# Gated delta-rule scan: squared lengths of keys and queries summed into the bank of alpha and beta, both transposed raw, and GpSimd's products moved to other tokens

## The reference

```python
q = _l2norm((x @ Wq).reshape(b, s, H, D)) / math.sqrt(D)
k = _l2norm((x @ Wk).reshape(b, s, H, D))
v = (x @ Wv).reshape(b, s, H, D)
dt = softplus(x @ Walpha + dt_bias)
alpha = exp(-exp(A_log) * dt)
beta = sigmoid(x @ Wbeta)

def step(state, inp):
    q_t, k_t, v_t, a_t, b_t = inp
    state = a_t[..., None, None] * state
    stored = einsum('bhij,bhj->bhi', state, k_t)
    delta = b_t[..., None] * (v_t - stored)
    state = state + einsum('bhi,bhj->bhij', delta, k_t)
    return state, einsum('bhij,bhj->bhi', state, q_t)
```

## Time and profile before

| what | value |
|---|---|
| median of the runs | 2251.55 us (2251.38 to 2252.23) |
| profiled execution: its time, its span | 2256.53 us, 2254.7 us |
| busy in the span: PE, DVE, ACT, POOL | 74%, 80%, 66%, 59% |
| first and last chain instruction of the scan | 31.5 us, 606.0 us |
| mean granted TensorE clock | 0.844 |

### The profile page before, as it was taken

One profiled execution on the slowest core, in us unless ns is written; L12 is line 12 of the kernel. 1 busy time (PEld: TensorE's weight loads), 2 busy tenths in 40 slices (PEclk: granted clock), 3 DMA queues, 4 the chain that ended last, 5 costly groups with the idle time before them and its releaser, 6 DMA issues. The chain is left out here.

```text
span 2254.7 us, 51777 instructions
## 1 busy us (share of the span) xinstructions
PE 1673.6 (74%) x16844; PEld 1360.7 (60%) x16844; DVE 1794.9 (80%) x4769; ACT 1480.4 (66%) x3849; POOL 1335.4 (59%) x1497
## 2 busy tenths in 40 slices
PE   5778777787654599993899999999987469997000
PEld 2555555455552388882788888888877258886000
DVE  6999999999878677785899999999957957776221
ACT  5787878788544577771788888888873747775000
POOL 3555556565500355533899999999870045553774
PEclk8888888888756699995999999999985679998555
DMA  1001010010340033331111111111102013333322
GB/s 35 15 15 29 15 29 21 22 29 10 95 146 19 27 81 80 82 72 33 26 29 31 31 30 31 31 31 31 27 8 75 0 49 80 81 82 64 80 77 56
DMA packets 145827, 101.59 MB, mean 45 GB/s; under 512 B 22144, under 2 KB 134688, under 8 KB 145568
## 3 DMA queue, kind: packets, MB, share of 16 engines
q1 hardware_dynamic: 110880, 54.20, 8.7%
q0 software_dynamic: 17408, 35.69, 6.9%
q10 hardware_dynamic: 17280, 8.40, 1.3%
HBM read 53.63 MB, written 35.65 MB: 40 GB/s over the span
## 5 line engine op out<-in xcount | busy, mean ns | idle before, releaser
L1067 POOL DMA_INDIRECT ffn_xs<-normed,ffn_tokeni x288 | 274.2, 952 | 450.6 <-DVE posi L1444 252.5
L1854 POOL TENSOR_TENSOR att_pl<-att_p,att_ph 128x384 f16<-128x384 f32 x512 | 454.6, 916 | 53.6 <-ACT att_ph L2075 45.3
L326 POOL TENSOR_TENSOR sq<-states,qS 128x256 f32<-128x256 f32 x256 | 243.0, 949 | 236.9 <-DVE states L754 235.0
L573 ACT ACTIVATE decayed<-states,alpha 128x64 f32<-128x64 f32 x1024 | 272.1, 336 | 107.4 <-DVE states L754 105.4
L1274 ACT ACTIVATE ffn_h<-bank,b_cols 128x256 f32<-128x256 f32 x576 | 226.1, 474 | 129.6 <-PE bank L1162 118.7
L2182 DVE TENSOR_REDUCE att_mx<-bank 128x3 f32<-128x384 f32 x512 | 279.6, 551 | 36.3 <-PE bank L1911 32.5
L2072 ACT ACTIVATE att_p<-bank 128x384 f32<-128x384 f32 x512 | 252.0, 492 | 57.1 <-PE bank L1948 54.3
L403 PEld LDWEIGHTS bank<-sq,ident 128*128 128x128 f32 x1024 | 225.6, 251 | 46.0 <-issue 26.7
L2075 ACT ACTIVATE att_ph<-bank 128x384 f16<-128x384 f32 x512 | 253.3, 495 | 0.0
L403 PE MATMUL bank<-sq,ident 128*128 128x128 f32 x1024 | 247.7, 413 | 3.3 <-POOL sq L326 3.3
L1175 PE MATMUL bank<-w_h,ffn_hh 128*128 x1152 | 226.0, 224 | 12.7 <-issue 3.8
(11 more groups left out here) (340 smaller groups left out, 5057.8 us busy)
## 6 DMA issues: line engine op xcount, KB each, us to landing
slots<-ffn_ys SPq DMA_DIRECT2D x144, 128.0 KB
normed<-ffn_xn ACTq DMA_DIRECT2D x32, 256.0 KB, 2.3
att_qz<-att_qp SPq DMA_DIRECT2D x256, 32.0 KB
ffn_xs<-normed,ffn_tokeni POOLq DMA_INDIRECT x288
xin<-in_x SPq DMA_DIRECT2D x64, 64.0 KB, 2.0
xres<-in_x SPq DMA_DIRECT2D x64, 64.0 KB, 2.0
x<-x SPq DMA_DIRECT2D x64, 64.0 KB, 1.8
x_all<-x SPq DMA_DIRECT2D x8, 512.0 KB, 4.8
```

Source lines behind the costliest of these rows:

```text
L326: nc.gpsimd.tensor_tensor(sq[:, t, :].rearrange("p (h i j) -> p h i j", h=HL, i=D), states[:, t, :].rearrange("p (h i j) -> p h i j", h=HL ...
L573: ins = nc.scalar.activation(decayed[:, 64 * h:64 * h + 64], states[:, (t - 1) % TC, 64 * h:64 * h + 64], ACT.Copy, scale=alpha[p][:, t, h ...
L1067: pool.indirect_dma_start(xs[j % AHEAD][:, r, :], None, A["normed"], bass.IndirectOffsetOnAxis(ap=tokeni[:, BR * j + r:BR * j + r + 1], ax ...
L1854: nc.gpsimd.tensor_tensor(pl[:, h % RP, :], p32[:, h % RP, :], ph[:, h % RP, :], ALU.subtract).then_inc(low_done, 1)
```

## The change

**Norms.** The two matmuls into full banks are gone. `pick_k` and `pick_q` are 128x128 matrices with one column for each head, so the squared lengths land in the columns of the alpha and beta bank that were empty (each group's 32 hold 4 alpha, 4 beta, now 4 k and 4 q). dt_bias is added there too, by a matmul of one row. One transpose (`ab_scan`) brings all four. ScalarE's relu and logarithm then work on 128x128, its two exponentials on 128x64.

**Keys and queries** are transposed unscaled, straight from PSUM. The lengths enter through GpSimd: beta_k = minus_beta x krinv, beta_kk = beta_k x krinv, beta_v uses beta_k, mab uses beta_kk, and the new product q_scaled (128x512) scales the queries. z, minus_z and minus_abs_z on VectorE become one Abs on ScalarE and a factor -1 in the exponential.

**Places.** Nearly all slots move; gate goes from step 15 of the chunk before to step 5 of its own.

```diff
-    ab_scan=24, z=25, minus_z=26, minus_abs_z=27, z_pos=29, v_scan=28, u_plus_2=33, u_rec=34, beta_den=35, minus_beta=36,
-    s=37, s2=38, h15=39, h13=41, h11=42, h9=43, k_unit=44, h7=45, h5=46, h3=47, k_scan=48, log1p=49, dt=50,
-    decay_log=51, gate_log=52, q_unit=56, q_scan=60)
+    xn=16, v_scan=22, k_scan=24, q_scan=28, ab_scan=32, z_pos=33, u_plus_2=36, u_rec=37, beta_den=38, minus_beta=39,
+    s=40, s2=41, h15=42, h13=43, h11=44, h9=45, h7=46, h5=47, h3=48, log1p=49, dt=50, decay_log=51, gate_log=52)
...
-PREP_ACT_STEP = dict(xT=0, x_sq=1, x_log=2, x_rinv=3, k_sq=5, q_sq=6, u=7, beta_exp=7, k_relu=8, k_log=9, k_rinv=10,
-                     gate_abs=10, gate_exp=11, q_relu=11, gate_ln=12, q_log=12, q_rinv=13, alpha=13, gate_sig=14, gate_rows=15)
+PREP_ACT_STEP = dict(xT=0, x_sq=1, x_log=2, x_rinv=3, k_sq=5, q_sq=6, z_abs=8, u=8, beta_exp=8, n_relu=9, n_log=9,
+                     k_rinv=9, q_rinv=9, gate_abs=10, gate_exp=11, gate_ln=12, alpha=13, gate_sig=14, gate_rows=15)
-POST_ACT_STEP = dict(o_sq=5, o_log=8, o_rinv=9, x1=14)
+POST_ACT_STEP = dict(o_sq=5, o_log=7, o_rinv=7, x1=14)
-PREP_POOL_STEP = dict(beta_v=11, minus_alpha_beta=14, k_scaled=14, gate=15)
+PREP_POOL_STEP = dict(beta_k=10, beta_kk=10, beta_v=11, q_scaled=12, minus_alpha_beta=13, k_scaled=13)
+GATE_STEP = 5
-POST_POOL_STEP = dict(o_unit=9, o_gated=10)
+POST_POOL_STEP = dict(o_unit=8, o_gated=9)
...
-            def k_norm(i, p):
+            def decays_and_norms(i, p):
                 c = 2 * i + p
+                if c == 0:
+                    pe.wait_ge(picked, 2)
+                nc.tensor.matmul(ps_t[:, :], wab[:, :], xn[:, :], start=True, stop=False)
+                nc.tensor.matmul(ps_t[:, :], dt_row[:, :], ones_row[:, :], start=False, stop=False)
                 pe.wait_ge(prep_act, prep_at(PREP_ACT, c, "k_sq"))
-                pe.wait_ge(prep_dve, prep_at(PREP, c, "v_scan"))
-                nc.tensor.matmul(ps_n[:, :], head_ones[:, :], ksq[:, :], start=True, stop=True).then_inc(prep_pe, 1)
-
-            def q_norm(i, p):
-                c = 2 * i + p
-                pe.wait_ge(prep_act, prep_at(PREP_ACT, c, "k_relu"))
-                nc.tensor.matmul(ps_n[:, :], head_ones[:, :], qsq[:, :], start=True, stop=True).then_inc(prep_pe, 1)
+                nc.tensor.matmul(ps_t[:, :], pick_k[:, :], ksq[:, :], start=False, stop=False)
+                pe.wait_ge(prep_act, prep_at(PREP_ACT, c, "q_sq"))
+                nc.tensor.matmul(ps_t[:, :], pick_q[:, :], qsq[:, :], start=False, stop=True).then_inc(prep_pe, 1)
...
                 if ahead(i, p):
+                    decays_and_norms(*ahead(i, p))
                     gates(*ahead(i, p))
-                    k_norm(*ahead(i, p))
-                    q_norm(*ahead(i, p))
...
-                elif name == "k_unit":
-                    act_did("k_rinv")
-                    ins = v.tensor_tensor(kE[:, :], ps_k[:, :], krinv[:, :], ALU.mult)
                 elif name == "k_scan":
-                    need("k_unit")
-                    ins = v.transpose(kS[p][:, :], kE[:, :])
+                    act_did("k_sq")
+                    ins = v.transpose(kS[p][:, :], ps_k[:, :])
...
                 elif name == "q_scan":
+                    act_did("q_sq")
+                    ins = v.transpose(qR[:, :], ps_q[:, :])
```

More of the change, by code:

```diff
@@ L144, in scan @@
         outer = ps_d[:, HL * D:HL * D + SD]
-        poly, polyb, urec = (held(HL * D + SD + n * TC * HL) for n in range(3))
-        nz, dtt = urec, polyb
+        poly, dtt, urec = (held(HL * D + SD + n * TC * HL) for n in range(3))
         alpha, mab = ([sb(f"{n}{p}", [P, TC, HL]) for p in range(2)] for n in ("alpha", "mab"))
@@ L275, in prep @@
                 g = nc.gpsimd
[L276 to L281, removed]
+                if name == "beta_k":
+                    pool.wait_ge(prep_dve, prep_at(PREP, c, "minus_beta"))
+                    pool.wait_ge(prep_act, prep_at(PREP_ACT, c, "q_rinv"))
+                    ins = g.tensor_tensor(bk[:, :, :], mbeta[:, :, :], krinv[:, :, :], ALU.mult)
+                elif name == "beta_kk":
+                    pool.wait_ge(prep_pool, prep_at(PREP_POOL, c, "beta_k"))
+                    ins = g.tensor_tensor(bkk[:, :, :], bk[:, :, :], krinv[:, :, :], ALU.mult)
+                elif name == "q_scaled":
+                    pool.wait_ge(prep_dve, prep_at(PREP, c, "q_scan"))
+                    ins = g.tensor_tensor(qS[p][:, :].rearrange("p (th i) -> p th i", i=D),
+                                          qR[:, :].rearrange("p (th i) -> p th i", i=D),
+                                          qrinv[:, :, :].rearrange("p t h -> p (t h)").unsqueeze(2)
+                                          .to_broadcast([P, TC * HL, D]), ALU.mult)
                 elif name == "beta_v":
-                    pool.wait_ge(prep_dve, prep_at(PREP, c, "minus_beta"))
+                    pool.wait_ge(prep_pool, prep_at(PREP_POOL, c, "beta_k"))
                     ins = g.tensor_tensor(prod[p][:, :, :, D].rearrange("p t (h i) -> p (t h) i", i=D),
                                           vS[:, :].rearrange("p (th i) -> p th i", i=D),
-                                          mbeta[:, :, :].rearrange("p t h -> p (t h)").unsqueeze(2)
+                                          bk[:, :, :].rearrange("p t h -> p (t h)").unsqueeze(2)
                                           .to_broadcast([P, TC * HL, D]), ALU.mult)
@@ L290, in prep @@
                     pool.wait_ge(prep_act, prep_at(PREP_ACT, c, "alpha"))
-                    ins = g.tensor_tensor(mab[p][:, :, :], alpha[p][:, :, :], mbeta[:, :, :], ALU.mult)
+                    pool.wait_ge(prep_pool, prep_at(PREP_POOL, c, "beta_kk"))
+                    ins = g.tensor_tensor(mab[p][:, :, :], alpha[p][:, :, :], bkk[:, :, :], ALU.mult)
                 else:
@@ L298, in prep, with gate @@
                 ins.then_inc(prep_pool, 1)
+            def gate(i, p):
+                c = 2 * i + p
+                pool.wait_ge(prep_act, prep_at(PREP_ACT, c, "gate_rows"))
+                if c >= 2:
+                    pool.wait_ge(post_pool, prep_at(POST_POOL, c - 2, "o_gated"))
+                nc.gpsimd.tensor_tensor(gE[p][:, :], gR[:, :], gsig[:, :], ALU.mult).then_inc(gated, 1)
             def post(name, i, p):
@@ L329, in chunk @@
                         qb.to_broadcast([P, HL, D, D]), ALU.mult).then_inc(sq_ready, 1)
+                    if t == GATE_STEP:
+                        gate(i, p)
                     if behind(i, p):
@@ L621, in prep @@
                     ins = v.transpose(aS[:, :], ps_t[:, :])
-                elif name == "z":
-                    need("ab_scan")
-                    ins = v.tensor_tensor(z[:, :, :], aview[:, :, 0:HL], hl(dt_bias[:, :]), ALU.add)
-                elif name == "minus_z":
-                    need("z")
-                    ins = v.tensor_scalar(nz[:, :, :], z[:, :, :], -1.0, None, ALU.mult)
-                elif name == "minus_abs_z":
-                    need("minus_z")
-                    ins = v.tensor_tensor(nab[:, :, :], z[:, :, :], nz[:, :, :], ALU.min)
-                elif name == "k_unit":
-                    act_did("k_rinv")
-                    ins = v.tensor_tensor(kE[:, :], ps_k[:, :], krinv[:, :], ALU.mult)
-                elif name == "k_scan":
-                    need("k_unit")
-                    ins = v.transpose(kS[p][:, :], kE[:, :])
-                elif name == "q_unit":
-                    act_did("q_rinv")
-                    ins = v.tensor_tensor(qE[:, :], ps_q[:, :], qrinv[:, :], ALU.mult)
+                elif name == "k_scan":
+                    act_did("k_sq")
+                    ins = v.transpose(kS[p][:, :], ps_k[:, :])
                 elif name == "q_scan":
-                    need("q_unit")
-                    if not (isinstance(c, int) and c < 2):
-                        dve.wait_ge(sq_ready, (c - 1) * TC)
-                    ins = v.transpose(qS[p][:, :], qE[:, :])
+                    act_did("q_sq")
+                    ins = v.transpose(qR[:, :], ps_q[:, :])
                 elif name == "gate_log":
@@ L655, in prep @@
                 elif name == "z_pos":
-                    ins = v.tensor_scalar(zp[:, :, :], z[:, :, :], 0.0, None, ALU.max)
+                    need("ab_scan")
+                    ins = v.tensor_scalar(zp[:, :, :], aview[:, :, 0:HL], 0.0, None, ALU.max)
                 elif name == "u_plus_2":
                     act_did("u")
-                    ins = v.tensor_scalar(u2[:, :, :], u[:, :, :], 2.0, None, ALU.add)
+                    ins = v.tensor_scalar(poly[:, :, :], u[:, :, :], 2.0, None, ALU.add)
                 elif name == "u_rec":
                     need("u_plus_2")
-                    ins = v.reciprocal(urec[:, :, :], u2[:, :, :])
+                    ins = v.reciprocal(urec[:, :, :], poly[:, :, :])
                 elif name == "s":
@@ L694, in _ @@
             for name in PREP:
-                if name == "ab_scan":
```

(3 more changed lines are left out.)

90 lines of the change are left out of this document (49 added, 41 removed).

## The result

| | before | changed |
|---|---|---|
| median | 2251.62 us (2251.38 to 2252.23, 4 runs) | 2263.42 us (2262.23 to 2265.03, 4 runs) |
| profiled execution: time, span | 2256.53, 2254.7 us | 2264.4, 2262.6 us |
| first product of the scan | 31.52 us | 33.08 us |
| one chunk, mean of 14 | 36.19 us | 37.05 us |
| last product of the scan | 604.56 us | 617.22 us |

The changed kernel is slower: the ratio is 1.0054, with a 95% interval of 1.0041 to 1.0066, 11.8 us by the medians, where 9.7 us were forecast. The difference lies in the scan, whose last product comes 12.7 us later: 0.92 of that by the start of the 2nd chunk, 11.94 in the 14 chunks, -0.20 in the last. What follows the scan took 1645.4 us after 1650.1 in the two profiled executions; the one of before was itself 5 us over its median, and the spans therefore differ by only 7.9 us.

A forecast was written before the change was run, and what follows sets the result against it. VectorE's queue in the scan was taken as the bound. Chunks of 36.19 us gain +0.71 on average, times 14 = +9.9 us; with -0.2 for the rest, the median 2251.55 + 9.7 = 2261.2 us, range 2243 to 2269.

The forecast's parts named there:

- What a long and a short instruction cost: VectorE's queue in the scan: a 128x512 instruction between two links costs 0.47 us, a short one nothing.
- Token 9: Scan, VectorE: the short beta_den is held under GpSimd's ounit, +0.48 us a chunk (bounds 0 and 0.48).
- Token 10: Scan: sq comes first and delays the product, +0.34 us; og holds the square and the outer product, +0.58 us.
- Tokens 12 and 15: Scan: beta_v delays the next product by 0.08 us; kabS holds the product of token 15 by 0.42 us.
- The chunk's start: Scan: 0.67 us freed on VectorE becomes a longer wait in token 3 if centring is slow, three chunks in four.
- The rest: Prologue, first and last chunk, memsets and DMAs, ScalarE's steps beside the chain: -0.2 us in sum.
- (1): Rival, scan: beta_den slips past ounit, 6.7 us less, 2254.5 us, no change; chance 0.12.
- (3): Rival, scan: VectorE's short instructions meet neither ounit nor og, 14.8 us less, 2246.4 us, faster by 0.23%; chance 0.20.
- (4): Rival, VectorE: each short instruction counts, three times 0.21 us in 15 chunks, 9.5 us less, 2251.7 us; chance 0.04.
- (2): Rival, chunk's start: TensorE keeps its clock, 9.0 us less, 2252.2 us, no change; chance 0.12.
- (5): Rival, ab_scan in token 8: the summed bank comes late, 1 to 2 us a chunk lost, 2275 to 2290 us; chance 0.07.

## Why the prediction was right

The sign, the size and the places came out; 2261.2 was forecast, 2263.42 measured.

- **What a long and a short instruction cost**, 0.47 us and nothing: held. k_unit and q_unit did give their 0.94 us. The three runs with instructions added show both prices and the exception, the start of the chunk.
- **Token 9**, beta_den under ounit: 3.01 us against 2.99 expected. Shown by taking the output out of SBUF, and by the first chunk, where ounit is missing and the token lasts 2.50 us.
- **Token 10**: 2.77 against 2.80. The product was held for 0.28 us (0.34 expected), the square for 0.58. Shown by the square's second input.
- **Tokens 12 and 15**: the 0.08 us for beta_v were nothing (0.01; beta_v ends early enough), the 0.42 us for kabS were right (2.30 us). Tokens 4 to 15 take 28.31 us in all, where 28.36 were forecast.
- **The chunk's start**: the late kabS and the long first product went, and the time with them, to the decay of token 3. This step was right in kind. It was mis-sized in how often: not three chunks in four but all of them had the slow centring, 37.05 us each against 37.11 for such a one. That makes 11.9 us in 14 chunks instead of 9.9. The count for the kernel before, 4 slow chunks of 14 by their lengths, was also too plain: the centring took 2.05 us in 4, 1.9 in 2, 1.4 in 3 and 1.10 or so in 5.
- **The rest** was forecast at -0.2 us and came to +0.7: the first product 1.6 us later (1.3 forecast), the first chunk 0.6 us shorter instead of 1.1, the last one 0.2 instead of 0.4. gE no longer lies under the first product, but in the first chunk token 3 waits 1.01 us where it waited 0.30. These are two single executions: in the second profile of the changed kernel the first product comes at 32.01 us and the first chunk is 1.1 us shorter than before, so this paragraph is not settled to better than some 1.5 us. By the scan alone the forecast is 3.0 us short, by the medians 2.2.
- **Rivals.** That beta_den slips past (1), that both short instructions meet nothing (3) and that each instruction counts (4) are refuted by the profile, og starting 0.38 us into token 10 where rival 3 needed 1.1, and by the runs on beta_den, the square and the three short copies. That TensorE keeps its clock (2) is refuted by 14 chunks of 14; the run with the filled idle time shows what it would have been worth. The summed bank was not late (5): aS waits for nothing but in the prologue and first chunk.

In sum, what the change saves (0.94 on VectorE, 0.24 by an ounit moved out of the way of a product, 0.66 at the chunk's start) is more than given back: 1.4 us in tokens 9 and 10 and 0.42 in token 15, by products of GpSimd that lie where VectorE has something that cannot run beside them, and the start's 0.66 and 0.20 more by a chain that VectorE's speed does not shorten and whose TensorE part got slower through idling (from the last state to token 4 it is 8.76 us in every chunk, where it was 8.44 to 8.76, 8.56 on average). By the tokens that is -1.18 + 1.82 + 0.20 = 0.84 us a chunk; measured are 0.85.

## What to carry to other kernels

Before a product of GpSimd is moved to where VectorE has long work, look at the operands of the short work beside it. Here a VectorE product of two inputs in SBUF (the square, 0.22 to 0.80 us) and a tensor_scalar from SBUF to SBUF (beta_den, 0.18 to 0.72 us) waited to the end of it, though they have only 64 elements a partition, and held what was queued behind; with one input, or the output, in PSUM they took 0.21 and 0.22 us. A gain on one engine counts only up to the next wait for another chain, so add a dummy instruction there: where it costs nothing, as in token 1 here, taking one out gains nothing either. And work that lets TensorE finish earlier can make its next matmul slower, as the centring shows (1.10 to 2.05 us).

## What the runs showed of the hardware that was not expected

- The clock's fall costs two matmuls of the chain, not one: 1.22 us a chunk between 4.2 to 4.7 us of idle time and 0.6 or less, by 18 matmuls whose result nobody reads.
- Where GpSimd came first, VectorE's record ends 0.04 to 0.09 us after GpSimd's for a short instruction and 0.23 to 0.29 us after it for a 128x256 product; for one pair of instructions it is the same from chunk to chunk to 0.03 us. This is regular enough to plan tables by. Where the product came first, sq took 0.97 us instead of 0.72.
- The same kernels take 80 us less on two of the four sets of runs (2171.7 against 2251.6 and 2250.3 us for the kernel before), nearly all of it after the scan. In the expert layers GpSimd's gathers waited 138.8 us for TensorE in the one profile of the changed kernel and 1.2 in the other. Why was not tried; it is left open.
